# Copying all four quads' probability products out of PSUM on ScalarE, in a transformer block on one core

## What is computed

```python
qkv = x @ Wqkv + bqkv                                  # 16 heads of size 16
scores = q @ k.T / sqrt(16) + alibi_causal_bias        # -inf above the diagonal
x = layernorm(x + (softmax(scores) @ v) @ Wo + bo)
up, gate = x @ ternary(W_up).T, x @ ternary(W_gate).T  # 1024 wide
x = layernorm(x + (silu(up) * gate) @ ternary(W_down).T)
```

## Time and profile before

| | |
|---|---|
| time, median of 3 runs | 626.57 us (623.8 to 627.0) |
| the profiled execution | 621.73 us, span 620.0 us |
| mean granted clock of PE over the span | 0.987 |
| PE busy | 582.8 us (94% of the span) |
| DVE busy | 494.3 us (80%) |
| ACT busy | 318.8 us (51%) |
| POOL busy | 299.0 us (48%) |

### The profile page before, as it was taken

The page is one execution under the profiler, slowest core; times in us unless marked ns, Lnnn a source line. Parts: engine busy times, 40 slices in busy tenths (PEclk is TensorE's granted clock), DMA queues, the critical chain, the costliest instruction groups (busy, mean ns, idle before and its releaser), DMA issues.

```text
span 620.0 us, 13168 instructions
## 1 busy us (share of the span) xinstructions
PE 582.8 (94%) x4152; PEld 348.0 (56%) x4152; DVE 494.3 (80%) x1258; ACT 318.8 (51%) x593; POOL 299.0 (48%) x504
## 2 busy tenths in 40 slices
PE   6779888999999999999999999999999999999795
PEld 4344354654656555664656656574566646546474
DVE  5388968996799859988599868989599877993766
ACT  2129713558347645477246644476255753576152
POOL 1306695346265535465175534564264543554234
PEclk9799999999999999999999999999999999999989
DMA  6865715015451073603553073502554053600001
GB/s 173 278 171 206 212 44 167 23 52 158 128 159 52 3 238 110 161 1 107 164 158 80 1 217 114 174 3 75 163 161 110 1 183 89 205 1 4 34 1 35
DMA packets 47724, 68.49 MB, mean 110 GB/s; under 512 B 4857, under 2 KB 43641, under 8 KB 44793
## 3 DMA queue, kind: packets, MB, share of 16 engines
q1 hardware_dynamic: 47691, 68.08, 37.2%
HBM read 38.44 MB, written 29.36 MB: 109 GB/s over the span
## 4 chain that ended last, share of the span: by engine, by line
PE 78%; DVE 6%; ACT 5%; POOL 5%; issue 3%; DMA 2%; SPq 1%; POOLq 0%; DVEq 0%
PE ring L690 18%; PE max_bank L613 10%; PE acc L643 9%; PE ring L631 9%; PE acc L707 7%; PE ring L589 7%; PE ring L596 4%; ACT probs L764 4%; PE ring L667 4%; PE max_bank L616 2%; PE ring L651 2%; POOL probs L1034 2%; POOL tern_down L1077 1%; PE ring L676 1%; PE ring L579 1%
## 5 line engine op out<-in xcount | busy, mean ns | idle before, releaser
L764 ACT ACTIVATE probs<-ring 128x512 f32<-128x512 f32 x320 | 170.7, 606 | 46.0 <-PE ring L631 44.3
L1034 POOL TENSOR_SCALAR_AFFINE_SELECT probs<-probs 128x256 f32<-128x256 f32 (+1 forms) x320 | 120.5, 402 | 131.8 <-ACT probs L764 131.1
L888 DVE CUSTOM_DVE_ANT_0 max_bank<-max_bank,causal_wide 128x384 f32<-128x384 f32 (+1 forms) x256 | 157.1, 636 | 15.7 <-PE max_bank L613 13.1
L613 PE MATMUL max_bank<-k_stack,q_stack 112*128 112x384 bf16 (+3 forms) x512 | 131.8, 304 | 6.9 <-DVE neg_max L888 3.1
L1070 POOL TENSOR_TENSOR hidden_lo<-hidden,hidden_hi 128x512 f16<-128x512 f32 (+1 forms) x72 | 75.2, 1050 | 63.8 <-ACT hidden_hi L795 63.5
L631 PE MATMUL ring<-q_stack,k_stack 114*128 114x512 bf16 (+3 forms) x512 | 103.7, 300 | 1.5 <-DVE attn L913 0.5
L783 ACT ACTIVATE gating<-ring,tanh_scale 128x512 f32<-128x512 f32 (+1 forms) x72 | 45.9, 639 | 74.6 <-PE ring L690 74.5
L643 PE MATMUL acc<-probs,v_ones 128*32 128x512 f32 (+3 forms) x1024 | 79.9, 438 | 2.8 <-POOL probs L1034 2.8
L613 PEld LDWEIGHTS max_bank<-k_stack,q_stack 112*128 112x128 bf16 x512 | 50.0, 98 | 45.2 <-DVE neg_max L888 15.4
L892 DVE TENSOR_REDUCE neg_max<-max_bank 128x2 f32<-128x512 f32 (+1 forms) x96 | 63.7, 685 | 10.7 <-PE max_bank L616 9.1
L631 PEld LDWEIGHTS ring<-q_stack,k_stack 114*128 114x128 bf16 x512 | 43.8, 97 | 48.2 <-issue 17.0
(11 more groups left out here) (105 smaller groups left out, 887.9 us busy)
## 6 DMA issues: line engine op xcount, KB each, us to landing
q_stack<-qk_scratch SPq DMA_DIRECT2D x15, 768.0 KB, 6.0
k_stack<-k_slots SPq DMA_DIRECT2D x15, 768.0 KB, 7.6
qk_scratch<-qk_parts SPq DMA_DIRECT2D x16, 384.0 KB, 3.0
k_slots<-qk_parts SPq DMA_DIRECT2D x16, 384.0 KB, 2.6
xin<-x_dram SPq DMA_DIRECT2D x8, 512.0 KB, 3.6
qk_scratch<-qk_parts SPq DMA_DIRECT2D x16, 256.0 KB, 3.3
k_slots<-qk_parts SPq DMA_DIRECT2D x16, 256.0 KB, 2.3
res<-x_dram SPq DMA_DIRECT2D x8, 512.0 KB, 3.4
```

The source lines that it names most:

```text
L613: mm = pe.matmul(o, q_stack[0:MAX_ROW, 4 * g + h, P * tile:P * (tile + 1)], k_stack[0:MAX_ROW, 4 * g + h, 0:width], start=True, stop=tile ...
L764: rg.drained(act.activation(probs[:, g % 2, n, :], rg.bank(step)[:, :], ACT.Exp), step)
L888: dve.tensor_tensor_reduce(scores, scores, causal_wide[:, SEQ - width:SEQ], -1.0, LOWEST_START, ALU.add, ALU.min, neg_max[:, g, first_col: ...
L1034: return pool.affine_select(out=v, in_=v, compare_op=ALU.is_ge, fill=0.0, base=0, pattern=([[0, blocks]] if blocks > 1 else []) + [[1, P]] ...
```

## The change

The instruction that empties `acc` for quads 2 and 3 moves from DVE's program to ACT's, at the same place of the lists. ACT now has 32 such copies, DVE none. What each waits for and what it raises stay as they were.

```diff
 # ACT's program
-                    elif kind == "pv" and step[1] < 2 and step[2] == TT - 1:
+                    elif kind == "pv" and step[2] == TT - 1:
                         g = step[1]
                         at_least(act, acc_filled[g % 2], 3, b, g // 2 + 1 - acc_skipped(name))
                         act.activation(pv_t[:, g % 2, :], acc[g % 2][:, :], ACT.Copy).then_inc(acc_drained[g % 2], 1)
 # DVE's program
-                    elif kind == "pv" and step[1] >= 2 and step[2] == TT - 1:
-                        g = step[1]
-                        at_least(dve, acc_filled[g % 2], 3, b, g // 2 + 1 - acc_skipped(name))
-                        dve.tensor_copy(pv_t[:, g % 2, :], acc[g % 2][:, :]).then_inc(acc_drained[g % 2], 1)
```

## The result

| | before | after |
|---|---|---|
| median of 22 runs each | 624.59 us (619.92 to 627.83) | 628.54 us (624.6 to 632.1) |
| ratio to before | | 1.0066, 95% interval 1.0046 to 1.0086 |
| profiled span | 620.0 us | 626.4 us |
| mean granted clock of PE | 0.987 | 0.973 |

The account below looks back on a forecast made before the run. PE, busy 94%, was taken to set the pace. Terms of +2.4 (FIRST), +0.5 (SECOND) and -0.6 (seven copies of quad 3) gave +2.3, so 628.8 us from a median of 626.57, range 624.8 to 631.0.

Parts of the forecast that it names:

- `pv.3.0` late by 2.1: End of FIRST: the last selects wait for DVE's long instructions, so pv.3.0 starts at about 79.2, 2.1 late.
- L1077 without its 2.15: POOL in FIRST: L1077 starts later but without 2.15 under DVE's L1010, so it ends near 84.5 as before.
- `var_eps` comes 1.6 later: DVE at the end of FIRST: the layernorm of batch 0, with L827, comes 1.6 late, at 90.8.
- `var_eps` held to the end of POOL's instruction: FIRST into SECOND: L827 falls inside POOL's L1082 and DVE is held until 94.12; the first take ends at about 94.15.
- FIRST was put at +2.4: Quad 2 of FIRST, the largest term: x1t.1 at 101.1 against 98.73, +2.4; upper bound +3.5 to 4.
- the 6.5 from that take: PE after FIRST: from the first take to the end of two matmuls before x1t.0 stays 6.5, putting x1t.0 at 100.65.
- this wait swallows the rest: PE before x1t.1: its 1.22 wait for ln1 swallows the rest of the 4.1, leaving +2.4.
- SECOND: Quad 2 of SECOND: 0.3 lost by a later exponential and 0.2 by ln2 against POOL's selects; +0.5 (0.3 to 0.8).
- The later turns: Quad 3 of SECOND, LOOP and SEVENTH: seven copies each end 0.094 sooner on PE's path; 0.6 gained, bounds 0 and 0.7.
- an overlap in `ln1`: Rival, clearly slower: DVE and POOL also meet in ln1, FIRST costs 4.4, sum +4.3, 630.9; chance 0.1.
- the cheaper copies: Rival, a little faster: copies are simply cheaper and FIRST's selects still pass; -0.3, 626.3; chance 0.2.
- DVE as the bound: Rival, clearly faster: DVE bounds the kernel and freeing 11.1 shows, 615.5 if all on the path; chance 0.05.

Follow-up runs that it names:

- e1: Changed kernel with the copy of quad 2 of FIRST back on DVE, the other 15 copies on ACT; ratio to the kernel before 0.9996.
- e2: Kernel before with only the copy of quad 2 of FIRST moved to ACT; ratio to the kernel before 1.0057.
- e3: Changed kernel with a useless DVE reduction of about the same length in the old place of FIRST's quad 2 copy; ratio to the kernel before 0.9980.
- e4: Changed kernel with 11 unused matmuls on PE before pv.3.0 of FIRST; ratio to the kernel before 1.0076.
- e5: Changed kernel with POOL's third instruction of the third ternary weight moved from the end of FIRST behind split.3 in SECOND; ratio to the kernel before 1.0000.
- e8: Kernel before with ternary.1 of FIRST moved behind nt_out.2 on DVE; ratio to the kernel before 1.0126.
- e7: Changed kernel with both POOL's third ternary instruction moved behind split.3 of SECOND and 11 unused matmuls before pv.3.0 of FIRST; ratio to the kernel before 0.9983.
- e6: Changed kernel with FIRST's quad 2 copy back on DVE and POOL's third ternary instruction moved behind split.3 of SECOND; ratio to the kernel before 0.9956.

## Why the prediction was right

The mechanism was right, and the net time too; the size of its largest term was half of what it turned out to be.

**The place and the sequence.** The main term of the forecast was a loss at the copy of quad 2 of FIRST, through a gap on DVE that POOL's selects need. e1, e2 and e3 show that: the loss goes when this copy goes back, comes when it alone is moved, and goes when the gap is filled otherwise. Term by term, counted from that copy's start:

- `pv.3.0` late by 2.1: measured (80.78 - 76.48) - (77.13 - 74.89) = 2.06.
- L1077 without its 2.15: measured 5.45 (L1073 now), and POOL's chain is not later. It ends 19.28 after the copy (95.76 - 76.48); in the kernel before it was 19.23 (94.12 - 74.89).
- `var_eps` comes 1.6 later: measured (94.02 - 76.48) - (89.21 - 74.89) = 3.2. The missing 1.7 is the clock, with which `pv.3` took 4.05: in e4, where `pv.3` takes 2.36, it comes (88.52 - 72.66) - 14.32 = 1.5 later. For the end of `var_eps` this changed nothing: it is 19.30 after the copy in the changed kernel and in e4. That is why it lasted 1.76 and not the 3 that I had forecast, and 3.44 in e4.
- `var_eps` held to the end of POOL's instruction: 95.78 against 95.76.
- `ln1` no longer held: 1.38 in place of 3.42, and 1.38 again in e5 to e8.

**The term that was mis-sized.** FIRST was put at +2.4 and measured +4.8, above even its upper bound of +3.5 to 4. Two things are missing in it.

The first take behind `var_eps` doesn't end with it but starts then: 95.70, 0.66 more. I had read from the earlier trace rows that the take can run beside an open `var_eps`; that held for a wait of 0.6 only.

And the 6.5 from that take to the end of the two matmuls before `x1t.0` didn't stay 6.5. In the kernel before its PE work began and went on so:

```profile
90.08 0.28 PE L613 MATMUL max_bank<-k_stack,q_stack 112*128 112x256 bf16 x1
...
92.08 1.03 PE L596 MATMUL ring<-wqkv,x_t 128*128 128x256 f32 x4
```

From the first matmul behind the take to the end of those two it was 95.92 + 0.60 - 90.08 = 6.4 before and is 104.07 + 0.60 - 96.43 = 8.2 after, 1.8 more, which with 0.66 makes the missing 2.4. PE's clock stood at 0.53 of full in the window 98 to 101, after the wait of 1.70; the four matmuls of `v.1` took 1.91 there in place of 1.03, for one. Not all of the 1.8 is the clock: in e5 and e7, with the clock at 1.00 there, the same work took 6.8. So some 1.4 goes with the low clock. The other 0.4 comes with a gap of 0.27 on DVE ahead of its instruction at 97.94, for which the trace names no releaser. It is there in e5 and e7 too; its cause is open.

The sentence "this wait swallows the rest" was right. I had no clock term at all, though the clock fell after both waits that I forecast, stayed up in `pv.3` when the first was filled (e4), and stayed up later when the second was gone (e5, e7).

**SECOND.** I gave +0.5; it was +0.05. The timeline of the changed kernel (it answers to the earlier trace rows):

```profile
157.57 1.56 DVE L812 TENSOR_SCALAR y<-z,mean_var,rstd 128x256 f32<-128x256 f32 x4 [3.29 <-POOL rstd L1061]
...
159.06 0.60 ACT L768 ACTIVATE pv_t<-acc 128x512 f32<-128x512 f32 x1
...
159.56 0.59 ACT L764 ACTIVATE probs<-ring 128x512 f32<-128x512 f32 x1
160.31 0.41 POOL L1030 TENSOR_SCALAR_AFFINE_SELECT probs<-probs 128x256 f32<-128x256 f32 x1 [0.42 <-ACT probs L764]
...
160.77 2.36 PE L643 MATMUL acc<-probs,v_ones 128*32 128x512 f32 x32 [0.34 <-POOL probs L1030]
```

The exponential starts 0.50 after the copy, not 0.60 (0.29 before): ACT begins it 0.10 before the copy's end. And `ln2`, moved ahead of the copy as forecast, has left the last select alone, which takes 0.41 in place of 0.54. `pv.3.0` is late by (160.77 - 159.06) - (154.35 - 152.70) = 0.06. My lower bound, 0.3, was too high.

**The later turns.** I forecast -0.6 for seven copies of quad 3. Six of them lie in the two last stretches of the table, which are 0.41 + 0.09 = 0.50 shorter: 0.08 each, against 0.09. `at.0` on ACT cost nothing.

**The sum and its luck.** Forecast +2.3, measured about +4 (624.59 x 0.0066 = 4.1, and 4.3 by the traces). That 628.8 lies so near the 628.54 measured is luck: the forecast change was 1.8 too small, and the median of three that it was built on, 626.57, was 2.0 above that of 22 runs. I gave "slower by over 0.5%" only 0.2, and the mechanism that I named for it, an overlap in `ln1`, is not what happened: `ln1` was free. With 1.4 for the clock and 0.66 for the take the sum would have been +4.4, 0.7%. Of the rivals, the cheaper copies exist and are worth 0.5 us; DVE as the bound is refuted by e3, which gives DVE work back and is faster.

The Trainium skill's rule ("SBUF — State Buffer", Who interferes with whom) that issue order decides who blocks, for the whole instruction, agrees with the traces in both directions here: a select of POOL that came second lasted 2.34, where the free ones last 0.3 to 0.4 (changed kernel), and DVE's L1008, when it came second, lasted 5.59 in place of 1.31 (e8).

## What to carry to other kernels

Here a short instruction between two long ones of VectorE was the time in which GpSimd got two of its selects done. Before moving or removing such an instruction, look at GpSimd's rows beside it: the selects of 2.34 and 1.38, among others of 0.3 to 0.4, marked the place in the kernel before. And ask of each long elementwise instruction of GpSimd what small VectorE instruction will arrive during it, since all that is queued behind that one waits too. Moving one long instruction of GpSimd to a later place was worth more here (0.4%) than the 0.5 us that the move of the copies gave.

## What the runs showed that was not expected

- In the changed kernel the clock fell after PE's waits of 2.93 and 1.70; in the kernel before, with waits of up to 1.22 from 58 to 104, it stayed at 1.00, but in e3 it fell after the same 1.22. The first fall cost 1.7 in `pv.3` (4.05 against 2.36), which only mattered where nothing later set the end: e4 got it back and lost it in the next wait, e7 kept it.
- A stalled `var_eps` let the take behind it start 0.08 after it when it was held for 0.6 (0.78 long), but not when it was held for 1.6 or 3.3 (take 1.68 and 3.35 after it). Why is open.
- In the profiles of e5 and e6, SEVENTH was 1.3 longer than in the kernel before (69.06 and 69.15 against 67.86), in e4 0.4 longer, and in e4 and e7 one turn of LOOP was 0.8 to 0.9 longer. Each time PE waited for a DMA where it didn't in the kernel before: 1.14 for one of the row maxima in e5 and e6, 0.75 and 0.89 for one in LOOP in e4 and e7, 0.94 for one of the keys in SEVENTH in e4. e7 has the same late instruction as e5 and e6 and no such wait in SEVENTH, so that edit alone doesn't bring it; what does is open. These waits are about as large as the effects that one profile is asked to show. The row of e6:

```profile
558.26 0.59 PE L631 MATMUL ring<-q_stack,k_stack 114*128 114x512 bf16 x3 [1.14 <-DMA q_stack<-max_parts]
```
